# A wavelet pyramid kernel: level 2 takes its odd columns from a GpSimd sum, and one store in eight is cut into five transfers

## What is computed

```python
for level in range(3):
    sh, sw = H // 2 ** level, W // 2 ** level
    temp = result[:, :, :sh, :sw]
    approx = conv3x3_same(temp, K)                     # K = outer([.25, .5, .25])
    result = result.at[:, :, :sh // 2, :sw // 2].set(approx[:, :, ::2, ::2])
...
x = x + wavelet_pyramid(group_norm(x), 3)
```

## Time and profile before

| what | us |
|---|---|
| median of 3 runs | 1298.64 (1297.83 to 1298.71) |
| the profiled execution, device time | 1298.75 |
| its span, first to last instruction | 1297.0 |
| first ScalarE pass over a group of the steady loop (L466, second group) begins at | 24.91 |
| last ScalarE pass over a group (L466, group 128) begins at | 1270.19 |
| busy: PE / DVE / ACT / POOL | 1207.8 / 1114.1 / 1139.6 / 478.7 |
| HBM read + written | 268.44 MB + 268.44 MB, 414 GB/s over the span |

### The profile page before, as it was taken

The page is one execution under the profiler, slowest core; times in us unless marked ns, Lnnn a source line. Parts: engine busy times, 40 slices in busy tenths (PEclk is TensorE's granted clock), DMA queues, the critical chain, the costliest instruction groups (busy, mean ns, idle before and its releaser), DMA issues.

```text
span 1297.0 us, 22951 instructions
## 1 busy us (share of the span) xinstructions
PE 1207.8 (93%) x7168; PEld 837.0 (65%) x7168; DVE 1114.1 (86%) x1664; ACT 1139.6 (88%) x1282; POOL 478.7 (37%) x1318
## 2 busy tenths in 40 slices
PE   5999999999999999999999999999999999999995
PEld 2666666666666666666666666666666666666664
DVE  5889889889889899899898888888888888898883
ACT  4998998998998998998998898889988889898995
POOL 4433433433433433433433343333333333333431
PEclk9999999999999999999999999999999999999998
DMA  9999999999999999999999999999999999999996
GB/s 385 395 416 424 423 422 424 423 423 423 424 423 423 423 423 423 423 424 422 424 422 422 423 424 421 422 421 408 418 421 417 407 419 416 407 416 423 411 397 257
DMA packets 106507, 537.01 MB, mean 414 GB/s; under 512 B 8192, under 2 KB 8192, under 8 KB 73728
## 3 DMA queue, kind: packets, MB, share of 16 engines
q1 hardware_dynamic: 53248, 268.45, 50.5%
q10 hardware_dynamic: 53248, 268.45, 49.9%
HBM read 268.44 MB, written 268.44 MB: 414 GB/s over the span
## 4 chain that ended last, share of the span: by engine, by line
PE 55%; ACT 30%; issue 11%; ACTq 2%; POOL 1%; DVE 0%; DVEq 0%; POOLq 0%
PE l_ps L373 17%; PE l_ps L376 17%; ACT xs L505 16%; PE l_ps L382 8%; ACT l L478 6%; PE l_ps L425 4%; ACT l L493 4%; PE var_ps L404 3%; ACT squares L466 2%; PE l_ps L427 2%; PE l_ps L426 2%; PE l_ps L428 2%; ACT l L477 2%; ACTq L515 1%; ACT junk L461 0%
## 5 line engine op out<-in xcount | busy, mean ns | idle before, releaser
L466 ACT ACTIVATE squares<-xs,negm 128x4096 bf16<-128x4096 f32 x128 | 474.8, 3710 | 4.1
L258 POOL TENSOR_TENSOR l<-l,col_fix 128x4 f32<-128x4 f32 x128 | 158.3, 1237 | 765.0 <-ACT l L478 765.0
L314 DVE SCALAR_TENSOR_TENSOR h<-xs 128x2048 f32<-128x2048 f32 x128 | 295.5, 2308 | 12.4 <-DMA xs<-x_dram 8.4
L322 DVE SCALAR_TENSOR_TENSOR h<-xs,h 128x2040 f32<-128x2040 f32 x128 | 291.5, 2277 | 0.0
L505 ACT ACTIVATE xs<-xs,negmr,r_plus 128x2048 f32<-128x2048 f32 x128 | 267.8, 2092 | 0.0
L301 DVE SCALAR_TENSOR_TENSOR xs<-l_ps,r,xs 64x256 f32<-64x256 f32 x256 | 123.0, 481 | 123.3 <-PE l_ps L428 121.5
L500 ACT ACTIVATE xs<-xs,negmr,r_plus 128x1024 f32<-128x1024 f32 x128 | 157.8, 1233 | 44.3 <-issue 44.3
L328 DVE SCALAR_TENSOR_TENSOR a<-h 128x1024 f32<-128x1024 f32 x128 | 157.8, 1233 | 4.4
L373 PE MATMUL l_ps<-a,w_odd 128*64 128x256 f32 x512 | 158.8, 392 | 0.0
L376 PE MATMUL l_ps<-a,w_odd 128*64 128x256 f32 x512 | 158.8, 392 | 0.0
L376 PE MATMUL l_ps<-a,w_even 128*64 128x256 f32 x512 | 152.3, 379 | 0.0
(11 more groups left out here) (88 smaller groups left out, 2404.5 us busy)
## 6 DMA issues: line engine op xcount, KB each, us to landing
xs<-x_dram SPq DMA_DIRECT2D x256, 1024.0 KB, 12.7
y_dram<-xs ACTq DMA_DIRECT2D x256, 1024.0 KB, 12.1
```

Of the source, the lines that this page charges most:

```text
L258: nc.gpsimd.tensor_tensor(col, col, col_fix[:, b], ALU.add).then_inc(l1_fixed, 1)
L314: nc.vector.scalar_tensor_tensor(h1[:, b], v[:, :, 0:W:2], 2.0, v[:, :, 1:W:2], ALU.mult, ALU.add).then_inc(h1_part, 1)
L322: nc.vector.scalar_tensor_tensor(h1[:, b, :, 1:W1], v[:, :, 1:W - 2:2], 1.0, h1[:, b, :, 1:W1], ALU.mult, ALU.add, accum_out=hsum[:, b:b + ...
L466: nc.scalar.activation(squares[:], xs[:, u % SLOTS, :], ACT.Square, bias=negm[:, b:b + 1], accum_out=sumsq[:, b:b + 1]).then_inc(sumsq_rea ...
```

## The change

Two edits that touch different engines.

First, GpSimd makes a tensor `pairs`, each odd column of level 1 plus the odd column on its left, 4 x 128 columns on 128 partitions, in one operation for a group. `l1` gets two columns of zeros ahead of each row (`PAD`), so that the first column's left neighbour reads as zero. The operation stands in GpSimd's step u after L252 and works on group u-1. It waits for `l2_ps_ready` of group u-3 and sets a new semaphore `pairs_ready`. Level 2 then has four matmuls instead of six: two of the even columns, a wait for `pairs_ready`, two of the pairs.

Second, the store of slot 3, one of eight, is issued as five transfers instead of two. The upper half, 128 partitions x (2 channels x 1024 columns), becomes channel 0 (128 x 1024), the first row of channel 1 (128 x 512), and the second row of channel 1 in two transfers of 119 and 9 partitions (x 512). The lower half is as before. The waits on that slot's semaphore count five stores.

```diff
@@ -16,8 +16,10 @@
 RPP = 2
 QUAD = CG * RPP
 SLOTS = 8
+SPARED = 3
 LAG = 1
 LAG_L3 = 2
+PAD = 2
 
 
 def pyramid_kernel(nc: bass.Bass, x: bass.AP, out: bass.AP):
@@ -53,7 +55,10 @@
         xs = sb("xs", [P, SLOTS, ROWS * W])
         h1 = sb("h1", [P, 2, ROWS, W1])
         a1 = sb("a1", [P, 2, HALVES, CG, W1])
-        l1 = sb("l1", [P, 2, CG, RPP, W1])
+
+        l1_pad = sb("l1_pad", [P, 2, CG * RPP, PAD + W1])
+        l1 = l1_pad[:, :, :, PAD:].rearrange("p b (c s) w -> p b c s w", c=CG)
+        pairs = sb("pairs", [P, 2, CG * RPP, W2])
         l2 = sb("l2", [P, 2, CG, W2])
         squares = sb("squares", [P, ROWS * W], BF16)
 
@@ -109,6 +114,7 @@
         l1_ps_ready = sem("l1_ps_ready")
         l1_ready = sem("l1_ready")
         l1_fixed = sem("l1_fixed")
+        pairs_ready = sem("pairs_ready")
         scaled = sem("scaled")
         l1_added = sem("l1_added")
         l2_ps_ready = sem("l2_ps_ready")
@@ -128,6 +134,10 @@
         def later(base, k, n):
             return not isinstance(base, int) or base + k >= n
 
+
+        def stores_of(slot):
+            return 5 if slot == SPARED else HALVES
+
         def rows(slot):
             return xs[:, slot, :].rearrange("p (r w) -> p r w", w=W)
 
@@ -148,7 +158,7 @@
         def _(sp):
             def load(lap, slot):
                 if later(lap, 0, 1):
-                    sp.wait_ge(x_stored[slot], 16 * HALVES * lap)
+                    sp.wait_ge(x_stored[slot], 16 * stores_of(slot) * lap)
                 for f in range(HALVES):
                     sp.dma_start(half_of(slot, f), x_half[f][lap, slot]).then_inc(x_loaded[slot], 16)
 
@@ -157,7 +167,7 @@
                     load(lap, slot)
 
             for slot in range(SLOTS):
-                sp.wait_ge(x_stored[slot], 16 * HALVES * LAPS)
+                sp.wait_ge(x_stored[slot], 16 * stores_of(slot) * LAPS)
 
         @block.gpsimd
         def _(pool):
@@ -177,6 +187,7 @@
 
             for w in (w1_prev, w1_even, w1_odd, w1_above, w2_first, w2_second, w3_odd, w3_keep):
                 nc.gpsimd.memset(w[:], 0.0)
+            nc.gpsimd.memset(l1_pad[:].rearrange("p b r w -> p (b r) w")[:, :, 0:PAD], 0.0)
             nc.gpsimd.memset(mean_w[:], -0.5 / N)
             nc.gpsimd.memset(var_w[:], 1.0 / N)
             nc.gpsimd.memset(col_t[:], -0.25)
@@ -234,6 +245,15 @@
                 pool.wait_ge(r_ready, n + 1)
                 nc.gpsimd.tensor_tensor(r_plus1[:, c], r[:, c], one[:], ALU.add)
                 nc.gpsimd.tensor_tensor(negmr[:, c], negm[:, c], r[:, c], ALU.mult).then_inc(coef_ready, 1)
+
+
+            def add_pairs(base, k):
+                b = k % 2
+                if later(base, k, 2):
+                    pool.wait_ge(l2_ps_ready, base + k - 1)
+                odd = l1_pad[:, b]
+                nc.gpsimd.tensor_tensor(pairs[:, b], odd[:, :, PAD + 1:PAD + W1:2], odd[:, :, PAD - 1:PAD + W1 - 2:2],
+                                        ALU.add).then_inc(pairs_ready, 1)
 
             def step(lap, u):
                 base = lap * SLOTS
@@ -251,7 +271,9 @@
                     nc.gpsimd.tensor_tensor(negm_e[:, c], negm[:, c], edge[:], ALU.mult)
                     nc.gpsimd.tensor_tensor(col_fix[:, b], negm[:, c].to_broadcast([P, TOP]), col_t[:],
                                             ALU.mult).then_inc(negm_e_ready, 1)
-
+                if exists(base, k):
+                    add_pairs(base, k)
+                if exists(base, u):
                     pool.wait_ge(negm_e_ready, n + 1)
                     pool.wait_ge(l1_ready, n + 1)
                     col = l1[:, b].rearrange("p c s w -> p (c s) w")[:, :, 0]
@@ -410,12 +432,13 @@
                 if later(base, u, 2):
                     pe.wait_ge(l2_added, base + u - 1)
                 dst = l2_ps[b][:, 0:CG * W2].rearrange("p (c w) -> p c w", c=CG)
-                src = l1[:, b]
-                for s, (plain, twice) in enumerate(((w2_first, w2_first2), (w2_second, w2_second2))):
-                    nc.tensor.matmul(dst, twice[:], src[:, :, s, 0:W1:2], start=s == 0, stop=False)
-                    nc.tensor.matmul(dst, plain[:], src[:, :, s, 1:W1:2], start=False, stop=False)
-                    last = nc.tensor.matmul(dst[:, :, 1:W2], plain[:], src[:, :, s, 1:W1 - 2:2], start=False,
-                                            stop=s == 1)
+                even = l1[:, b, :, :, 0:W1:2]
+                pair = pairs[:, b].rearrange("p (c s) w -> p c s w", c=CG)
+                nc.tensor.matmul(dst, w2_first2[:], even[:, :, 0], start=True, stop=False)
+                nc.tensor.matmul(dst, w2_second2[:], even[:, :, 1], start=False, stop=False)
+                pe.wait_ge(pairs_ready, base + u + 1)
+                nc.tensor.matmul(dst, w2_first[:], pair[:, :, 0], start=False, stop=False)
+                last = nc.tensor.matmul(dst, w2_second[:], pair[:, :, 1], start=False, stop=True)
                 last.then_inc(l2_ps_ready, 1)
 
             def level3(base, k):
@@ -511,8 +534,18 @@
                 act.wait_ge(scaled, n + 1)
                 act.wait_ge(l1_added, n + 1)
                 act.wait_ge(l2_added, n + 1)
-                for f in range(HALVES):
-                    nc.scalar.dma_start(out_half[f][lap + back, slot], half_of(slot, f)).then_inc(x_stored[slot], 16)
+                dst, src = out_half[0][lap + back, slot], half_of(slot, 0)
+                if slot != SPARED:
+                    nc.scalar.dma_start(dst, src).then_inc(x_stored[slot], 16)
+                else:
+
+
+                    most = 7 * 17
+                    nc.scalar.dma_start(dst[:, 0], src[:, 0]).then_inc(x_stored[slot], 16)
+                    nc.scalar.dma_start(dst[:, 1, 0:W], src[:, 1, 0:W]).then_inc(x_stored[slot], 16)
+                    nc.scalar.dma_start(dst[0:most, 1, W:], src[0:most, 1, W:]).then_inc(x_stored[slot], 16)
+                    nc.scalar.dma_start(dst[most:P, 1, W:], src[most:P, 1, W:]).then_inc(x_stored[slot], 16)
+                nc.scalar.dma_start(out_half[1][lap + back, slot], half_of(slot, 1)).then_inc(x_stored[slot], 16)
 
 
             def store_half(lap, k, f):
```

## The result

The changed kernel takes **1321.75 us** (median of five runs, 1316.55 to 1321.96) against 1298.64 us of the kernel before in the same session (1297.83 to 1299.0). The ratio is 1.0166, with a 95% interval from 1.0145 to 1.0187. The prediction said 1328, range 1286 to 1352, slower with 0.66. Its sign and its size came out.

What follows compares the result with a forecast made beforehand. Before, one slow transfer share bounds; after, VectorE, held by GpSimd's sum. 51.7 us outside the steps + 126 x 10.12 - 3 = 1323.8; 1.75 around the span and 3 for issues give 1328.5, said as 1328; range 1286 to 1352.

Steps and rivals of the forecast that it cites:

- The bound before: Transfers: one lagging share of sixteen bounds from about 700 us at 10.11 us a group; the compute loop needs 9.72.
- Part 1: Level 2 on TensorE: two matmuls fewer, gain taken 0, at most 1.5 us a step without ScalarE's scaling as cover.
- Part 2: The sum on GpSimd: holds VectorE 1.1 us a step, of which 0.7 is free, giving steps of 10.12 us.
- a hold of 1.25 - 0.14 = 1.1 us: GpSimd's sum, taken as 1.25 us, blocks VectorE for all but 0.14 us of its length.
- the second rival: VectorE: short hold or lucky place of the sum, 0.78 to 0.9 us; time 1289 to 1302 us; chance 0.08.
- the first rival: VectorE: the sum holds nobody, or under 0.78 us; the slow share bounds at 10.03, 1289 us, faster; chance 0.27.
- 126 x 10.12: The loop's 126 steps at VectorE's circle of 9.02 us plus the hold: 1275.1 us of the forecast.
- Part 3: Slot 3's store in five pieces: slow share to 10.03 us a group if it loses rows; issues taken as 0.
- that case: Slot 3's store: slow share among the seven that get more rows, 10.21 us a group, 1311 us; chance 0.05.
- the change turns a kernel bound by transfers into one bound by VectorE: Whole loop: transfers need at most 10.03 us a group, VectorE's circle with the hold 10.12.
- ScalarE's `issue` waits gone: Sign of a right forecast: ScalarE's waits between store issue and scaling, 45 times and 44.3 us before, disappear.
- The 3 us outside the steps: End of the kernel: the 3 us in which one share works alone go, as no backlog builds up.

Runs made afterwards that it cites:

- e1: Only the first edit (GpSimd's sum, four level 2 matmuls) on the kernel before, stores in two transfers: 1299.56 us against 1299.84, ratio 0.9998.
- e4: As e1, but GpSimd fills `pairs` with zeros by memset instead of adding, and waits for `l2_ps_ready` two operations earlier: 1299.16 us, ratio 0.9991.
- e2: Only the second edit (slot 3's store in five transfers, 119 and 9 partitions among them) on the kernel before: 1318.64 us, ratio 1.0145.
- e8: Kernel before with only slot 3's store cut, its last 128 columns of channel 1 as 123 and 5 partitions: 1299.4 us against 1300.6, one run.
- e9: Kernel before with only slot 3's store cut, its last 128 columns of channel 1 as 114 and 14 partitions: 1309.67 us against 1300.6, one run.
- e5: As e2, but all five transfers over 128 partitions, channel 1's second row in two halves of 256 columns: 1304.63 us against 1300.03, ratio 1.004.
- e3: Kernel before with slots 0 to 5 storing 128 columns over 127, 122, 123, 124, 125 or 114 partitions and a rest: 1516.69 us, one run.
- e6: Kernel before with slots 1, 3 and 5 storing 128 columns over 123, 122 or 124 partitions and a rest: 1378.71 us, one run.
- e10: Kernel before with slot 3's load in six transfers, its last 192 columns as 123, 3 and 2 partitions: 1310.27 us against 1298.92, ratio 1.0092.
- e7: As e1, with GpSimd's sum made a second time into a tensor that nobody reads: 1405.23 us, ratio 1.0809.

## Why the prediction was right or wrong, point by point

**The bound before** was read rightly: one lagging share, about 10.1 us a group, 0.16 us a step of slack in the compute loop. The 10.11 comes from 38 of ScalarE's steps, which are uneven; the loads give 10.08. e1 confirms the slack: 0.12 us more in every step, nothing in the time.

**Part 1, two matmuls worth 0:** right (e4).

**Part 2, the sum.** Right: it is exclusive with VectorE, gets in at the seam, `pairs_ready` costs next to nothing (TensorE waits 1.8 us in all for it), and the step is VectorE's circle plus the hold. 9.02 + 0.84 = 9.86 against steps of 9.84. By the rule of the Trainium skill, "SBUF — State Buffer", section "Who interferes with whom", that is what is to be expected, and e1 with its sum and the two steps of e4 with its memset agree. Wrong: the term "a hold of 1.25 - 0.14 = 1.1 us". The sum takes 1.06 us. The Trainium skill's figure ("GPSIMD Engine Reference", section 3.1) had given an estimated 1.12, and the prediction set it aside for the middle of two far bounds. About 0.2 us of the sum costs VectorE nothing. A hold of 0.84 us lies in the band of the second rival (0.78 to 0.9 us, chance 0.08), though for a shorter sum and not for a lucky place, and e1's 1299.56 us lies in its 1289 to 1302. It is a hair under the point of 0.85 that the first rival named (its own working, 1245.3 / 126 - 9.02, gives 0.86). So the term "126 x 10.12" is 126 x 9.84, 35 us less. That is 1293 us, and the transfers hide it.

**Part 3, the store.** Wrong in its central assumption: "on the slow share that would be 10.11 - 0.08 = 10.03 us a group if it is among those that lose". It is among the seven that carry 17 rows each of the 119-partition transfer (e2, e8, e9). The prediction gave that case 0.05, on the Trainium skill's remark ("DMA: Bandwidth & Descriptors", "Latency and other measured facts") about which engines are usually slower, 7 and 15; here it is share 3 or 4 if few shares are the lowest-numbered, and in any case one of the seven, and the measurement decides. No row told either way, so its chance had to be nearer to the seven in sixteen that counting gives. Its price was 0.10 us a group, which gave 1311 us. Of the 20 us between the profiled runs of e2 and of the kernel before, 12.8 have arisen when the store of group 120 lands, so that term was sized rightly. The other 7.3 arise in the last eight groups, where slot 3's pair of steps takes 12.5 and 11.3 us instead of 9.72 each; the prediction had no term for that, and what else is in them stays open. The 3 us that the changed kernel is longer than e2 are there when the 16th group has landed. For the issues the prediction takes 0 in its text and 3 us in its sum; e5 lost 5, e8 nothing.

**The statement that "the change turns a kernel bound by transfers into one bound by VectorE"** failed with both. The store edit alone costs nearly the whole loss and the sum alone nothing, so the kernel is still bound by transfers. So did "ScalarE's `issue` waits gone", "steps of about 10.1 us from the start" and "GB/s near 414 and even": the mean of 10.09 us is made of 9.84 and 11.3. The 3 us outside the steps went, but into the last two steps. "Stores of slow and quick shares landing close together" failed too: in the ninth lap one share brings slot 3's store in 21.1 to 33.7 us after the issue, the others by 17.0. TensorE waiting for `h1` in most steps was right, 127 times against 11 before. It is no sign of a hold, though: e4 has none, and there TensorE waits 127 times as well (85.2 us), since level 2 is shorter.

So the time of 1328 was near 1322 by luck, because two errors met: a hold too long by 0.26 us a step, and a store that costs 19 us alone instead of 3. The range and the chances held for a cause that had 0.05.

## What to carry to other kernels

Two resources that each run near the bound have to be priced each alone, and then the longer taken; a total that comes out right proves neither. When bytes are moved between shares of a transfer, first find out which share is late: the arrival times of the single increments show that there is one, and trial transfers over few shares narrow it down, as long as they are so few that the loop isn't slowed (e8 and e9, not e3 and e6). Small rows and few shares have a price of their own, which can eat a gain of one per cent of the bytes at once. And a GpSimd operation that reads SBUF should be costed at nearly its length on VectorE wherever VectorE is busy with two SBUF inputs.

## What the runs showed of the hardware that was not expected

- Small rows are dear on the lagging share. Eight of 1 KiB cost it 1.8 to 1.9 us (e5), eight of 2 KiB 2.7 us and seventeen of 2 KiB 4.5 us (e2). Half the bytes for eight rows save a third of the time.
- One late share holds the engine that issues. An ordinary store's two issues take 1.13 us early in the kernel before and 3.80 at 1061 us. In a store of several transfers the hold falls on whichever meets it: the nine partitions behind the 119 took 1.97 us in one lap of the changed kernel and 0.31 in another, where the 1 MiB transfer behind them took 2.46. Few shares bring the hold on by themselves: five issues with 127 partitions on one share took up to 12.2 us although no share lagged otherwise (e3), and three small ones on SP 1.3 us early and 15 late (e10).
- A GpSimd operation that reads held VectorE's instructions with two SBUF inputs for its length less 0.2 us (0.84 of 1.03 in one step), a second one right behind it for 0.77 more (e7), and a memset of the same size not at all (two steps of e4). Under an instruction that reads PSUM and one SBUF input the same sum held nobody (1.04 us under L323, 0.98 for the pair).
